# A triangle-update kernel on one core: a tick table per stage, centring on GpSimd, chunk preloads, gate spreading on ScalarE, a second buffer for turned pairs

## What is computed

```python
def layer0(z):                      # mask, ln_w, ln_b, W_*, b_*
    zn = layer_norm(z)
    a = (zn @ W_ap + b_ap) * sigmoid(zn @ W_ag + b_ag) * mask
    b = (zn @ W_bp + b_bp) * sigmoid(zn @ W_bg + b_bg) * mask
    return z + einsum('bikc,bkjc->bijc', a, b) @ W_z + b_z

def layer1(x):
    xn = layer_norm(x)
    left  = sigmoid(xn @ left1)  * (xn @ left2)
    right = sigmoid(xn @ right1) * (xn @ right2)
    p = layer_norm(einsum('nsre,nkre->nske', left, right))
    g = sigmoid(xn @ gate)
    return x + einsum('nrse,ez->nsrz', p, out_w) * g
```

## The kernel before, in words

| stage | ticks | content |
|---|---|---|
| z | 53, then 8 | steps 0 to 51 with one half a tick (from tick 5); then 8 ticks with two halves each |
| contraction 0 | 16 | one unit a tick, steps 52 to 63 in the first 12 |
| quadrants 4 and 5, with contractions 1 and 2 behind them | 16 + 16 each | a step and two halves a tick, then units |
| quadrant 6, contraction 3 | 16 + 16 | steps alone, then units |
| quadrant 7, contraction 4 | 32 + 16 | two halves a tick, a step every other tick |
| quadrants 8 and 9, contractions 5 and 6 | 16 + 16 each | a step and two halves a tick |
| quadrants 10 and 11, contraction 7 between | 16 + 16 + 16 + 6 | steps alone |

## Time and profile before

### The profile page before, as it was taken

One profiled execution on the slowest core, in us unless ns is written; L12 is line 12 of the kernel. 1 busy time (PEld: TensorE's weight loads), 2 busy tenths in 40 slices (PEclk: granted clock), 3 DMA queues, 4 the chain that ended last, 5 costly groups with the idle time before them and its releaser, 6 DMA issues.

```text
span 1250.1 us, 26342 instructions
## 1 busy us (share of the span) xinstructions
PE 896.1 (72%) x9820; PEld 839.1 (67%) x9820; DVE 837.5 (67%) x1907; ACT 580.1 (46%) x834; POOL 526.6 (42%) x361
## 2 busy tenths in 40 slices
PE   2544444444657787988886888889888988866875
PEld 1434443443557786987875888889888988856864
...
GB/s 77 74 102 101 93 77 115 173 176 160 236 177 272 272 252 192 93 247 275 180 260 187 193 80 175 220 252 221 215 284 178 98 272 239 268 203 204 35 186 202
DMA packets 173237, 228.71 MB, mean 183 GB/s; under 512 B 11064, under 2 KB 109624, under 8 KB 171064
## 3 DMA queue, kind: packets, MB, share of 16 engines
...
## 4 chain that ended last, share of the span: by engine, by line
PE 30%; DVE 27%; issue 16%; ACT 14%; POOL 6%; DMA 5%; SPq 2%; DVEq 0%; ACTq 0%; POOLq 0%
PE bank L975 16%; DVE stats L804 7%; ACT xt L624 5%; POOL rstd L549 5%; DVE xc L837 4%; PE ps_w L1005 4%; DVE split L844 4%; DMA chunk<-xt 3%; PE bank L955 3%; ACT sig L600 3%; PE bank L956 2%; ACT chunk L642 2%; DVE lhs L778 2%; DVE xin L817 2%; PE ps_x L1016 2%
## 5 line engine op out<-in xcount | busy, mean ns | idle before, releaser
L549 POOL TENSOR_TENSOR rstd<-var,minus_half 128x8 f32<-128x8 f32 x192 | 328.0, 1709 | 685.5 <-DVE var L812 685.5
L975 PE MATMUL bank<-rhs,lhs 128*128 128x128 f32 x2048 | 242.9, 280 | 23.2 <-POOL lhs L543 10.2
L975 PEld LDWEIGHTS bank<-rhs,lhs 128*128 128x128 f32 x2048 | 238.0, 196 | 24.1 <-issue 19.9
L1016 PE MATMUL ps_x<-ident_b,split 128*128 128x128 bf16 x1024 | 98.2, 253 | 187.6 <-DVE split L844 182.0
L600 ACT ACTIVATE sig<-bank 128x512 f32<-128x512 f32 x256 | 152.7, 597 | 132.1 <-PE bank L956 130.4
L1016 PEld LDWEIGHTS ps_x<-ident_b,split 128*128 128x128 bf16 x1024 | 76.8, 114 | 203.0 <-DVE split L844 176.4
L606 ACT ACTIVATE split<-xc 128x504 bf16<-128x504 f32 x128 | 79.7, 623 | 256.7 <-DVE xc L837 256.7
L955 PE MATMUL bank<-w_rhs,chunk 128*128 128x128 bf16 x1024 | 160.2, 246 | 25.2 <-DVE lhs L778 14.3
L955 PE MATMUL bank<-w_lhs,chunk 128*128 128x128 bf16 x1024 | 156.7, 242 | 28.8 <-DMA chunk<-xt 19.4
L1005 PE MATMUL ps_w<-w_out,opair 128*128 128x128 f32 x1024 | 146.5, 288 | 23.6 <-DVE split L851 20.3
L955 PEld LDWEIGHTS bank<-w_lhs,chunk 128*128 128x128 bf16 x1024 | 138.5, 151 | 35.2 <-DMA chunk<-xt 22.2
...
## 6 DMA issues: line engine op xcount, KB each, us to landing
...
xin<-in_x_dram SPq DMA_DIRECT2D x128, 256.0 KB, 3.9
...
```

What stands on the lines that cost most here:

```text
L549: g.tensor_tensor(rstd[:, m % 2], var[:, m % 2], minus_half[:, :], ALU.pow).then_inc(rooted, 1)
L975: last = mm(bank[:, n], operand["lhs"][:, kh, c, :], operand["rhs"][:, kh, c, :], start=kh == 0, stop=kh == HALVES - 1)
L1016: last = nc.tensor.transpose(ps_x[:, h, n, :], split[:, h, n].rearrange("p a c -> p (a c)"), ident_b[:, :])
```

## The change

The hand-written lags are replaced by a table: for every kind of tick, each stage has its own lag, and each engine goes through its stages in one fixed order. With it:

- `centre` runs on POOL for z steps 0 to 21 and 56 to 63 and for all x steps; on DVE for z steps 22 to 55 and all p steps. Before, POOL had the even z steps from 52 on, half of quadrant 6, all of quadrant 7, and half of quadrants 8 and 9. `root` comes last in a POOL tick, and POOL's masks of the z steps wait for the `normalise` of step t - 2.
- In z, `gates` of a half stand one tick ahead of its `make`; `normalise` stands ahead of `low`.
- z steps go up to 55 ahead of contraction 0, and the last 8 are spread over 11 of its ticks.
- Six chunk loads (`EARLY`, numbers 24 to 29) go into free parts of `quad` at once, instead of through the ring of two.
- `spread_gate` moves from DVE to ACT; the last 16 gate loads alternate between two buffers.
- In quadrants 6 and 7 the turned pairs alternate between `opair` and a second buffer in the place of the masks.
- DVE's masks come in 16 units for each contraction instead of 8 groups.
- For p steps, `turn` comes in the tick of the step instead of two later; the list ends with 8 ticks instead of 6.

```diff
+Z_LAGS = dict(load=-2, stats=0, variance=0, root=0, centre=1, norm=1, high=1, low=2, turn_x=2, xt=3,
+              col=3, store=4, project=3, gates=4, make=5)
...
-    for t in range(53):
-        tick(t if t < 52 else None, [t - lag] if t >= lag else [])
+    for m in range(3 * STEPS):
+        tick("z", m, [m])
+    for m in range(3 * STEPS, Z_LATE - 2):
+        tick("last z", m)
     for i in range(8):
-        tick(None, [48 + 2 * i, 49 + 2 * i], spill=(0, 0, i // 2) if i % 2 else None)
...
+EARLY = range(DIRECT + GROUPS, DIRECT + GROUPS + 6)
+def ring_before(n):
+    return n - 8 if n in (DIRECT + 14, DIRECT + 15) else n - 2
...
 def centre_on_pool(m):
-    kind = step(m)[0]
-    quadrant = m // STEPS
-    if kind == "z":
-        return m >= 52 and m % 2 == 0
-    if kind == "x":
-        return quadrant == 7 or (quadrant == 6 and m % 2 == 0)
-    return quadrant < 10 and m % 2 == 0
+    return m < Z_EARLY or Z_LATE <= m < P_BASE
...
+        PAIRED = X_BASE + 2 * STEPS + 1
+        opair_2 = masks[:, 0].rearrange("p h n -> p (h n)").rearrange("p (n k) -> p n k", k=P)
+        def opair_of(m):
+            return opair_2 if PAIRED <= m < P_BASE and m % 2 else opair[:, :, :]
...
                 pool.wait_ge(stats_done, after(m))
+
+                pool.wait_ge(normed, after(m - 1))
...
+                for m in due("centre", t):
+                    if centre_on_pool(m):
+                        centre(m)
+                for m in due("residual", t):
+                    add_residual(m)
                 for n in pool_masks_at(t):
+                    if t < MASK_TWO:
+
+                        pool.wait_ge(normed, after(t - 2))
                     mask_operand(n)
+                for m in due("root", t):
+                    root(m)
...
+            def spread_gate(m):
+                w = (m - P_BASE) // 2
+                act.wait_ge(gchunk_landed[w % 2], 16 * (w // 2 + 1))
+                act.wait_ge(gate_mm, after(2 * w - 3))
...
+                a.activation(by_vector(gspread[w % 2]), by_group(gchunk_of(w)), ACT.Copy).then_inc(gate_spread, 1)
...
+                halves = due_halves("make", t)
+                for h in halves[:-1]:
+                    make(h)
+                for m in due("stats", t):
+                    statistics(m)
+                for h in halves[-1:]:
+                    make(h)
...
+                for m in due("variance", t):
+                    variance(m)
+                for m in due("scale", t):
+                    scale(m)
+                for m in due("norm", t, "p"):
+                    normalise(m)
+                for m in due("centre", t):
+                    if not centre_on_pool(m):
+                        centre(m)
+                for m in due("add", t):
+                    add(m)
+                for m in due("norm", t, "zx"):
+                    normalise(m)
+                for m in due("low", t):
+                    low(m)
...
             for t in range(T_END):
+                for m in due("turn_x", t):
+                    turn_x(m)
+                for m in due("gate", t):
+                    gate_product(m)
+                if unit_at(t):
+                    contract(*unit_at(t))
+                for h in due_halves("project", t):
+                    project(h)
```

More of the change, by code:

```diff
@@ new lines @@
+LATE_Z_LAGS = dict(Z_LAGS, turn_x=3, xt=4, col=4, store=5)
+LAGS = {
+    "z": Z_LAGS,
+    "last z": LATE_Z_LAGS,
+    "z in contraction": LATE_Z_LAGS,
+    "second half": dict(LATE_Z_LAGS, project=0, gates=0, make=1),
+    "x with chunks": X_LAGS,
+    "x alone": dict(X_LAGS, load=0, add=1, keep=2, stats=2, variance=2, root=2, centre=3, norm=3,
+                    low=4),
+    "x every other tick": dict(X_LAGS, stats=4, variance=4, root=4, centre=5, norm=5, high=5, low=6,
+                               turn_x=7, xt=7, store=8),
+    "p with chunks": P_LAGS,
+    "p alone": dict(P_LAGS, gate_out=1, spread=-1, gate_load=-4),
+}
```

391 lines of the change are left out of this document (172 added, 219 removed).

## The result

The changed kernel takes **1057.23 us** (median of 4 runs, 1056.49 to 1060.67) where the one before takes 1250.59 in the same comparison: a ratio of 0.846, with a 95% interval of 0.844 to 0.848. The forecast was 1071, with a range of 1040 to 1140. The profiled execution took 1056.53 us, its span is 1054.7.

The account below looks back on a forecast made before the run. No engine fills the span: a loop of waits bounds z, DVE quadrants 5 and 8, PE the contractions and nearly quadrant 7. Gains of 122+10+6+9+12+8+13 = 180 us from 1251.9 give 1072, median 1071; range 1040 to 1140.

Parts of the forecast that it names:

- The opened loop in z: z: gates a tick ahead of make let the wait path span two ticks; 122 us gain with contraction 0.
- The double ticks: End of z, 8 ticks with two halves: 30 us instead of 40, six chunks being loaded ahead.
- Contraction 0: Between z and x: 44 us instead of 52, with 8 steps in it instead of 12; bounds 37 and 50.
- DVE's own sum: DVE's work per step: in z 3.5 us with centre, 2.8 without; in quadrants 4 and 5, 4.0.
- the lock: Rival, whole kernel: wide POOL and DVE instructions shut each other out; +230 us, 1301; chance 0.05.
- POOL's floor in early z: Early z: root and centre make 2.7 us, 3.2 with handoffs; 3.3 us a step taken.
- Transfers as the next limit: Late z 3.8, quadrants 4 and 5 4.2 us a step at 312 GB/s; as slower rival 1119 us, chance 0.17.
- quadrants 4 and 5: First x quadrants: 4.2 us a step, gaining 10 and 6 us after deductions for the edges.
- Quadrant 6: Steps without halves, POOL about 3.2 us a step: 51 us instead of 60, gain 9.
- Quadrant 7: make around the statistics shortens PE's waits: 6.4 us a step instead of 7.1, gain 12, bounds 0 and 15.
- Quadrants 8 to 11: p steps: DVE loses the spread copy; 4.25, then 3.2 us a step; gains 4, 4, 8 and 5 us.
- A longer loop: Rival, z: an unseen chain over ACT and PE costs two ticks and halves the step gain; 1146 us, chance 0.13.

Follow-up runs that it names:

- gates_same_tick: Changed kernel with the gates of z put back into the tick of their make, all else left: 1176.36 us, ratio 0.942.
- before_open: Kernel before with only the make of z's halves, up to half 46, one tick later: 1173.43 us, ratio 0.940.
- half_chunks: Changed kernel with each ring load of a chunk cut to 64 of 128 partitions: 1054.62 us, ratio 0.844.
- ring_only: Changed kernel without the six early chunk loads, all going through the ring of two: 1058.0 us, ratio 0.846.

## Why the prediction held, and where its terms were off

**The opened loop in z** was right in place, and in size as a sum: 122 us predicted with contraction 0, 124.7 measured, and `gates_same_tick` gives 119 of it back with one number. That the sum came so near is in part luck. The steps up to tick 54 gained 106 us, where I had 96. The double ticks with the stretch up to the first unit gained 15.9, where I wrote 10; the 9 us from 351 to 360, in which PE stood waiting for a mask, were in my 412 but in none of my terms. Contraction 0 gained 3.2 and not 8. Two steps behind the loop were not as I put them. It also goes over PE, by `low` and `turn_x`. And where masks run, an opened loop does not give DVE's own sum by itself: `before_open` reaches 3.50 us a step up to step 22, and 4.57 behind it, since `normalise` is held by a mask. I had listed the lock as a rival for the whole kernel, and missed that the new order removes it from a place where it already cost something, once the loop is open.

**POOL's floor in early z** held: 3.3 predicted, 3.22 measured, with `root` and `centre` at 3.09. They are longer than the 2.7 of the earlier trace rows, since DVE now holds `root` back, and the handoffs are 0.13 and not 0.5. The two errors cancel: the number was right by luck, that POOL is full was not.

**Transfers as the next limit** were wrong, the 3.8 of late z and the 4.2 of quadrants 4 and 5. At 3.48 us a step late z moves 285 GB/s at a share of 0.90, and `half_chunks` hardly gains. The 312 GB/s that I called the busiest stretch of the trace were not: over contraction 2, from 617 to 645 us, the same kernel moved 342. By that figure a tick's 1.31 MB would have taken 3.8 us, below DVE's sum. The 3.5 us "of full use" from a share of 0.59 came near by chance: the share is no measure of how much more would go through. DVE's sum was the limit that I had right as a mechanism, and mis-sized: 3.84 in the timeline of quadrant 4, where I took 4.70 - 0.71 = 4.0. Quadrants 4 and 5 make 13 of the 15 us by which the whole gain was larger. In quadrant 4 only 2 of its 8 come from the steps (21.3 gained for 19). The rest is the edge, where I took 9 off and the longer contraction 1 took 3.4. In quadrant 5 the steps gained 15.5 for my 8, and contraction 2 took 4.0 for my 2.

**The double ticks** took 32.7 us and contraction 0 45.6, where I had 30 and 44. The loaded chunks, to which I gave part of this gain, have no share in it that `ring_only` could show.

**Quadrant 6** gained 0.70 us a step where I took 0.5, but 6.3 us with its contraction where I took 9: its steps gain the 9, and contraction 3 takes 33.9 us instead of 31.0, with more of the trailing steps in it. The second pair buffer, which I costed at nothing, carries 0.29 of the 0.70 in the mean, all of it in the first steps.

**Quadrant 7**: 6.4 predicted, 6.23 measured; 15.7 us is just above the upper bound of 15. That it comes from the two `make` around the statistics was argued and not tried.

**Quadrants 8 to 11** came out near the prediction in sum, and by luck, since the gain is not where I put it. Up to their contractions quadrants 8, 9 and 10 gained 0.1, 1.0 and 0.5 us; contractions 5, 6 and 7 gained 4.0 each, which no term of mine held. PE has less of the trailing steps to do in them. That `turn` of a p step now comes two ticks sooner fits this, but was not tried alone. From the first to the last statistics the steps did get shorter, by 2.9 us in quadrant 8 and by 8.0 in quadrant 10. The first statistics of quadrant 10 come later, though, 4.8 us behind contraction 6 instead of 1.5, and contraction 7 starts 7.2 us behind the last ones instead of 2.9. On DVE the spread copy was 0.68 of work and up to 1.1 of waiting; moving it is worth 6 us in the new order. `normalise` was held beside POOL's `centre` in 5 of 15 steps of quadrant 8 before and in 2 of 16 after.

**The rivals.** The lock did not come: `normalise` has a mean of 0.73 us over the kernel (0.76 before), and 17 of DVE's wide instructions are longer than 0.8 (50 before). Transfers did not set the pace. A longer loop was there, and it too was cut by the same tick.

## What to carry to other kernels

In an order written by ticks, follow each loop of waits and count the ticks it spans: its time divided by that count is the floor of a step. One tick more for one stage was worth 76 of 193 us by itself, and 119 on top of the rest of the change, which it first lets act. Only then ask which engine is full, and what stands beside what on DVE and POOL, since a duration measured beside the other engine contains its waiting; look at the least of a group as well as its mean or median. Split each gain at the borders of the stages too: a sum can be right while the time was saved elsewhere. Where a load goes into a buffer that a store empties, leave a tick between the two in the queue: issued too soon, the load holds up the next store.

## What the runs showed of the chip

DVE copies 128 x 2048 bf16 in 0.68 us, and in up to 1.76 beside POOL's two-input instructions; ACT takes 1.90 for the same. Holding is not only for wide instructions: a variance of 128 x 8 takes 0.62 instead of 0.16 us under POOL's `centre`, and POOL's `root` of 128 x 8 goes from 1.65 to 1.95 and 2.05 beside DVE's wide ones. This core, which runs alone, moved 409 GB/s over 9 us and 342 over 28, with the share of its DMA engines read as 1.02 and 1.01. The granted clock in early z went from 0.56, with PE busy 27.6 of 60 us, to 0.91, with 19.3 of 40; it was 0.60 again in `gates_same_tick`, with 18.0 of 40, and 0.59 in `before_open`, with 24.8 of 40.
